# Causal attention's row maxima in chunks of four heads, spread over both sequences' steps, with a reordered first stage

## The reference

```
h = layernorm(layernorm(x)); h = causal depthwise conv of width 3 (h); q, k, v = split(h @ attn_w)   # 16 heads of 8 dims
q, k = rotary(q), rotary(k)
scores = einsum('bhqd,bhkd->bhqk', q, k) / sqrt(8)
scores = where(causal, scores, -1e30)
p = softmax(scores)
x = x + einsum('bhqk,bkhd->bqhd', p, v) @ proj_w
x = x + moe(layernorm(x))          # 4 experts, the best one for each row
```

## Time and profile before

| | |
|---|---|
| runs, us | 349.03, 351.30, 351.62 (median 351.3) |
| span of the profiled execution, first to last instruction | 346.5 us |
| time of that execution outside the span | not shown by the page; the three runs are 2.5, 4.8 and 5.1 us above the span |
| TensorE busy | 321.4 us, 93% |
| VectorE busy | 240.7 us, 69% |
| ScalarE busy | 215.8 us, 62% |
| GpSimd busy | 121.6 us, 35% |
| shares of the chain that ended last | TensorE 58%, VectorE 25%, ScalarE 10%, issue 4% |

### The profile page before, as it was taken

The page is one execution under the profiler, slowest core; times in us unless marked ns, Lnnn a source line. Parts: engine busy times, 40 slices in busy tenths (PEclk is TensorE's granted clock), DMA queues, the critical chain, the costliest instruction groups (busy, mean ns, idle before and its releaser), DMA issues.

```text
span 346.5 us, 6818 instructions
## 1 busy us (share of the span) xinstructions
PE 321.4 (93%) x2406; PEld 228.1 (66%) x2406; DVE 240.7 (69%) x607; ACT 215.8 (62%) x633; POOL 121.6 (35%) x151
## 2 busy tenths in 40 slices
PE   7888999998999998988999999998999999999885
PEld 2336887664566544435654898995688687877774
DVE  4987766594899977852651464368788877887575
ACT  1478886165237364565668744855766676686994
POOL 3525563101630033330522161410586535535300
PEclk9999999999999999999999999999999999999999
DMA  7690000057777300009002002300100000000002
GB/s 207 204 264 2 2 0 2 6 161 218 214 240 195 81 2 0 2 9 340 25 8 78 0 17 70 84 2 1 55 15 18 0 2 0 3 1 0 2 0 63
DMA packets 21591, 22.46 MB, mean 65 GB/s; under 512 B 3606, under 2 KB 18358, under 8 KB 21558
## 3 DMA queue, kind: packets, MB, share of 16 engines
q1 hardware_dynamic: 19750, 19.93, 19.8%
q0 software_dynamic: 512, 1.05, 1.0%
q10 hardware_dynamic: 1296, 1.05, 0.9%
HBM read 14.22 MB, written 7.60 MB: 63 GB/s over the span
## 4 chain that ended last, share of the span: by engine, by line
PE 58%; DVE 25%; ACT 10%; issue 4%; DMA 1%; POOL 1%; ACTq 0%; DVEq 0%; POOLq 0%
PE PS L1312 49%; DVE mB L835 9%; PE PS L1366 6%; ACT big L1122 3%; ACT big L1288 3%; DVE big L669 2%; DMA X<-in_x 1%; DVE XN L625 1%; DVE big L642 1%; DVE mraw L634 1%; ACT big L1096 1%; DVE U L625 1%; DVE stats L614 1%; DVE mraw L658 1%; ACT big L1240 1%
## 5 line engine op out<-in xcount | busy, mean ns | idle before, releaser
L1312 PE MATMUL PS<-big 128*128 128x128 f32 (+10 forms) x592 | 94.7, 308 | 6.7 <-DVE big L642 1.7
L1312 PEld LDWEIGHTS PS<-big 128*128 128x128 f32 (+3 forms) x592 | 58.0, 150 | 38.3 <-issue 11.3
L511 POOL TENSOR_TENSOR big<-big,urec 128x1024 f32<-128x1024 f32 x24 | 45.6, 1898 | 62.8 <-DVE urec L676 45.6
L1122 ACT ACTIVATE big<-big 128x154 f32<-128x154 f32 x192 | 60.4, 319 | 6.7 <-DVE big L669 5.0
L1240 ACT ACTIVATE big<-PS 128x1024 f32<-128x1024 f32 (+3 forms) x64 | 42.2, 704 | 25.5 <-PE PS L1312 25.1
L835 DVE TENSOR_REDUCE mB<-PS 128x2 f32<-128x256 f32 (+5 forms) x90 | 50.1, 624 | 7.2 <-PE PS L1312 7.2
L1096 ACT ACTIVATE big<-PS 128x1280 f32<-128x1280 f32 (+2 forms) x30 | 32.6, 1091 | 32.5 <-PE PS L1366 30.0
L1312 PE MATMUL PS<-cstb 128*128 128x128 bf16 x192 | 37.8, 220 | 0.0
L1312 PE MATMUL PS<-kkC,XT 128*128 128x462 f32 (+1 forms) x96 | 36.0, 510 | 1.7 <-DVE big L669 1.7
L499 POOL TENSOR_TENSOR rstd<-ve,minus_half 128x4 f32<-128x4 f32 (+2 forms) x13 | 13.2, 1016 | 69.0 <-DVE ve L620 69.0
L1122 ACT ACTIVATION_READ_ACCUMULATOR big<-big 128x1 f32 x192 | 36.3, 189 | 0.0
(11 more groups left out here) (192 smaller groups left out, 489.4 us busy)
## 6 DMA issues: line engine op xcount, KB each, us to landing
scr_qk<-big SPq DMA_DIRECT2D x12, 384.0 KB, 3.5
big<-scr_qk SPq DMA_DIRECT2D x16, 288.0 KB
big<-in_wv SPq DMA_DIRECT2D x1, 2048.0 KB, 8.1
scr_x<-zrow SPq DMA_DIRECT2D x2, 448.0 KB, 6.5
scr_y<-big SPq DMA_DIRECT2D x2, 448.0 KB, 3.6
X<-in_x ACTq DMA_DIRECT2D x2, 256.0 KB, 3.8
big<-in_A_WoT ACTq DMA_DIRECT2D x1, 512.0 KB, 4.7
cw<-in_C_Wk SPq DMA_DIRECT2D x1, 512.0 KB, 5.3
```

Of the source, the lines that this page charges most:

```text
L511: pool.tensor_tensor(pn[:, 0:GH * P].rearrange("p (h k) -> p h k", h=GH), Pt[u % 3][:, :, 0:KM], r.to_broadcast([P, GH, KM]), ALU.mult).th ...
L1122: i = act.activation(Pt[u % 3][:, h, :], Pt[u % 3][:, h, :], ACT.Exp, accum_out=usum[:, u % 3, h:h + 1])
L1312: return pe.matmul(o, lhsT, rhs, start=start, stop=stop)
```

## The change

The maxima are made final by chunks c = 0..7 of four heads (8 m each) instead of by sequence. Only the first 20 m (`M0`) come before the steps; the other 44 are spread over steps 0 to 21 as a ring of 66 entries, three to a step: an m with one or two tiles of columns is one entry for both heads, a wider one is two entries. The ring has two banks (5 and 6). The reductions negate. GpSimd splits each chunk into three bf16 parts, one bf16 matmul turns the three together, ScalarE copies them, and SyncE stores them. The folds of `PREC` go with m = 2..19, one each. The five `hold_clock` matmuls between the sequences are gone. Sequence 0 is now transposed and normalised four heads at a time too, in steps 5, 9, 13, 17, and `turn_outputs` and `normalise_first` are gone. ScalarE issues the two loads of expert weights. In stage A the reciprocal of unit u-1 comes between the maximum and the clamp of unit u, transposes come before values, values are three units behind, VectorE makes the second half of the queries, constants are spread over units 0 to 4, nine of the `hold_clock` matmuls are gone, `turn("b")` comes before folds 3 to 5, folds 6 to 8 come after the first `queries_keys`, which no longer waits for the last `add_tile`.

```diff
@@ block.vector, units_A @@
+                        if u >= 1:
+                            row_sums(u - 1)
                         own.wait()
                         own(dve.tensor_scalar(umax[:, u % 2, :], mraw[:, u % 2, :], LEAST, None, ALU.max))
...
-                    if u >= 1:
-                        v = u - 1
-                        dve.wait_ge(unit_exp["A"], v + 1)
-                        dve.reciprocal(urec[:, v % 3, :], usum[:, v % 3, :]).then_inc(unit_rec["A"], 1)
-                    if u >= 4:
-                        add_tile("A", u - 4)
+                    else:
+                        row_sums(u - 1)
+                    if u >= 3:
+                        add_tile("A", u - 3)
...
@@ block.tensor, units_A @@
+                    if 2 <= u <= NT + 1:
+                        turn_weights("A", u - 2)
                     if u == 2:
                         pe.wait_ge(q4_ready, B)
                         hold_clock(OUT_BANK["A"], 8)
-                    elif u == 3:
-                        hold_clock(OUT_BANK["A"], 5)
-                    if u >= 4:
-                        weigh_values("A", u - 4, vwAm, vwAr)
-                    if 2 <= u <= NT + 1:
-                        turn_weights("A", u - 2)
+                    if u >= 3:
+                        weigh_values("A", u - 3, vwAm, vwAr)
...
             def second_gap():
+                turn("b", XN, (0,))
                 fold_C(F_UNIT[0], F_UNIT[1])
-                turn("b", XN, (0,))
...
-                else:
-                    pe.wait_ge(tile_added["A"], NT)
...
+        M0 = 20
+        M_STEPS = 22
+        S_CHUNK = (None, 0, 3, 7, 11, 15, 20, 23)
+        S_SPLIT = {2: 2, 6: 3, 10: 4, 14: 5}
+        RING = []
+        for m in range(M0, 64):
+            RING += [(m, (0, 1))] if m % QT < QT // 2 else [(m, (0,)), (m, (1,))]
+        def ring_bank(k):
+            return 5 + k % 2
...
+            def split_maxima(c):
+                pool.tensor_copy(mp[:, c % 2, 0], m).then_inc(m_part, 1)
+                pool.tensor_tensor(mr[:], m, mp[:, c % 2, 0], ALU.subtract).then_inc(part_step, 1)
+                pool.tensor_copy(mp[:, c % 2, 1], mr[:]).then_inc(m_part, 1)
+                pool.tensor_tensor(mp[:, c % 2, 2], mr[:], mp[:, c % 2, 1], ALU.subtract).then_inc(m_part, 1)
...
+            def ring_scores(k):
+                if k < 2:
+                    pe.wait_ge(s_max, M0)
+                else:
+                    pe.wait_ge(s1_max, k - 1)
...
             late = F_LATE
-            for m in range(32):
+            for m in range(M0):
                 scores_for_maximum(m)
-                if m >= 3 and m % 2 == 1 and late < F_BETWEEN:
+                if m >= 2 and late < len(PREC):
                     fold_C(late, late + 1)
                     late += 1
-            hold_clock(7, 5)
-            turn_maxima(0)
+                if late == F_MAX:
+                    turn_maxima(0)
...
-                    if s < S_MAX:
-                        scores_for_maximum(M_MERGE + 2 * s + pair)
-                if s >= 1 and s != 16:
+                    if s < M_STEPS:
+                        ring_scores(3 * s + pair)
+                if s >= 1:
                     outputs(s - 1)
...
+                if s < M_STEPS:
+                    ring_scores(3 * s + 2)
+                if s in S_CHUNK:
+                    turn_maxima(S_CHUNK.index(s))
+                if s >= 5 and s % QT == 1 and s != 21:
+                    turn_group(*divmod((s - 5) // QT, 4))
```

More of the change, by code:

```diff
@@ L251, in program @@
         F_VALUES = 42
-        F_BETWEEN = 46
+        F_MAX = 45
         def prec_jobs():
@@ L381, in program, with first_bank, ring_done @@
         PREA = [(kind, b, k) for b in range(B) for kind, k in (("vw", 0), ("vw", 1), ("vr", 0))]
[L383 to L388, removed]
+        def first_bank(m):
+            return (0, 2, 5)[(m - M0) % 3]
+        RING = []
+        for m in range(M0, 64):
+            RING += [(m, (0, 1))] if m % QT < QT // 2 else [(m, (0,)), (m, (1,))]
+        assert len(RING) == 3 * M_STEPS
+        def ring_bank(k):
+            return 5 + k % 2
+        def ring_done(c):
+            return sum(m < M_CHUNK * (c + 1) for m, _ in RING)
         def y_bank(n):
@@ L1370, in units_A @@
             def units_A(between):
-                for u in range(NT + 4):
+                for u in range(NT + 3):
                     if u < NT:
@@ L1546, in _, with turn_maxima, scores_of @@
             pe.wait_ge(consts_ready, 2)
-            def turn_maxima(b):
-                pe.wait_ge(*((s1_max, 2 * (64 - M_MERGE)) if b else (s_max, 32)))
-                if b:
-                    pe.wait_ge(m_part[0], 1)
-                pe.transpose(PS[0:HB * QT, 6, 0:P], mB[:, b].rearrange("p h t -> p (h t)"), ident).then_inc(m_turned, 1)
-            def scores_for_maximum(m):
+            def turn_maxima(c):
+                pe.wait_ge(m_part, 3 * (c + 1))
+                if c == 0:
+                    pe.wait_ge(preC_act, sum(j[2] for j in PREC[:F_MAX - 1]))
+                elif c == 1:
+                    pe.wait_ge(preC_act, N_PREC)
+                elif c == 2:
+                    pe.wait_ge(rwc_ready, 2)
+                elif c <= 5:
+                    pe.wait_ge(y_norm, c - 2)
+                elif c == 6:
+                    pe.wait_ge(attn_added, 1)
+                elif c == 7:
+                    pe.wait_ge(routed, 1)
+                mm(PS[0:3 * HG * QT, LN_BANK, M_AT:M_AT + P], mp[:, c % 2].rearrange("p a n -> p (a n)"), identb).then_inc(m_turned, 1)
+            def scores_of(b, h, qt, o):
+                w = (qt + 1) * P
+                mm(o, qs[b][0:SPLIT, h, qt * P:w], ks[b][0:SPLIT, h, 0:w], stop=False)
+                return mm(o[:, w - P:w], identb, mask_qk, start=False)
+            def scores_for_maximum(m):
+                hp, qt = divmod(m, QT)
+                if m % M_CHUNK == 0:
+                    pe.wait_ge(stack_ready[0][m // M_CHUNK], 32)
+                if m >= 3:
+                    pe.wait_ge(s_max, m - 2)
+                for j in range(2):
+                    i = scores_of(0, 2 * hp + j, qt, PS[:, first_bank(m) + j, 0:(qt + 1) * P])
+                i.then_inc(s_mm, 1)
+            def ring_scores(k):
+                m, heads = RING[k]
                 b, n = divmod(m, 32)
```

407 lines of the change are left out of this document (210 added, 197 removed).

## The result

The changed kernel took 344.51, 344.60, 345.59 and 347.59 us, median 345.1, beside 349.03, 349.48, 351.30 and 351.62 us (median 350.4) of the kernel before: ratio 0.9875, 95% interval [0.983, 0.9921], 1.25% faster. The forecast was 349.4 us, 0.6% faster, with "within 1%" likelier than "faster"; the interval reaches from 0.8 to 1.7%. The time lies in the forecast's range (344.5 to 353.5), but near its lower end.

What follows compares the result with a forecast made beforehand. TensorE's work was taken as nearly the bound everywhere. The terms -1.9 - 8.2 + 6.8 + 1.35 = -1.95 brought the span from 346.5 to 344.6 us; with 4.8 added, the median was 349.4, range 344.5 to 353.5.

Steps and rivals of the forecast that it cites:

- Stage A, -1.9: From the start to the second turn: 1.9 us gained, ends nothing and 3.2.
- The loop: Stage A: exponentials, reciprocal, clamp and subtractions form a cycle of 4.5 us a unit, longer than TensorE's 4.26.
- Ahead of the steps, -8.2: First maximum's matmul to first step: 20.6 us instead of 28.8, 8.2 gained, ends 9.8 and 6.2.
- Steps, +6.8: Steps 0 to 23: 62.8 us instead of 56.0, 6.8 lost, with 0.65 a period for all waits.
- the three terms: Steps 16 to 19, added to a period: masks 0.9 us, the normalised turn 0.5, the projection 1.0.
- Tail, +1.35: Behind step 24's first exponential: places known later and the bias matmul moved in, 1.35 us lost, ends 0 and 2.2.
- the 0.9: Tail: TensorE meets the 1.65 us later places of sequence 0's rows late by about 0.9 us.
- The waits vanish: Rival, steps: TensorE's lead absorbs the ring's waits (3.6 us) and half of step 20's block (0.9): 344.9 us; chance 0.26.
- the block of step 20: VectorE's addition and statistics, 2.8 us in one piece in step 20, of which TensorE sees 1.9 us as a wait.
- Two banks are too few: Rival, steps: ring entries wait behind VectorE's copy and normalisation, 1.25 us more a period: 356.3 us; chance 0.12.
- stage A gives nothing: Rival, stage A: a unit really takes 4.7 us through signals between engines, the 1.9 gained goes: 351.3 us; chance 0.12.
- The clock falls: Rival, stage A: without fillers the clock halves for one unit, 4.26 us doubles: 353.7 us; chance 0.03.

Runs made afterwards that it cites:

- The repeat: The changed kernel run again without any edit: median 347.8 us, ratio 0.9890 to the kernel before.
- the maxima alone: The changed kernel with the first stage as before, so only the maxima by chunks are new: 350.2 us, ratio 0.9945 to the kernel before.
- the reciprocal back: The changed kernel with stage A's reciprocal back behind the subtractions: 355.3 us, ratio 1.0102 to the kernel before.
- the folds back: The changed kernel with the second turns' folds where they were before the change: 346.8 us, ratio 0.9849 to the kernel before.
- stage A's fillers back: The changed kernel with the nine filler matmuls of the first stage put back: 348.3 us, ratio 0.9931 to the kernel before.
- the seventh: The changed kernel with eight unread matmuls where TensorE waits 1.67 us in step 21: 345.2 us, ratio 0.9864 to the kernel before.
- the kernels with fillers: The changed kernel with fillers in step 21, 345.2 us; the changed kernel with 24 maxima ahead of the steps and fillers in step 29, 344.4 us.

## Why the prediction was right and wrong

**Stage A, -1.9, measured -2.5 (-2.9 from the first maximum).** The loop was right: 4.46 us a unit. Wrong were two sizes. I let unit 7 end 0.3 us later than before, which my own terms did not give (1.2 lost, 1.4 given back); from unit 0's first maximum to unit 7's it took 31.19 us after and 31.47 before, 0.3 earlier, because the constants that left unit 0 gave back 1.1 (4.40 for 5.53) and the six units behind it cost 0.85 instead of 1.2. And the wait for the normalised rows, 1.2 in the sum, was 0.63. The stretch from queries to second turn (16.2 us) was as forecast. Wrong, too, was to book the reciprocal's new place as a cost alone: with it back in its old place the first m comes 5.8 us later. The sum did not depend on it.

**Ahead of the steps, -8.2, measured -8.35.** Right as a sum, 20.42 us for 20.6, with parts that cancel: TensorE is busy for 19.63 instead of 19.0, and waits for 0.8 instead of 1.6, since fold 45 does not wait.

**Steps, +6.8, measured +6.9.** Right as a sum, with errors that cancel. TensorE's idle time in a period was 0.28, not 0.65, so two banks were enough, but its work was larger: 9.5 to 9.6 us a period, and 39.5 instead of 38.8 us for steps 0 to 15. Steps 16 to 19 took 11.25 instead of 11.9 (9.7 and the three terms add up to 12.1), with no idle time at all. Steps 20 to 23 took 12.16 for 12.1; the wait in step 21 was 1.67 for 1.9. The forecast holds for an execution at full clock: with a dip the steps take 64.3 us, +8.4.

**Tail, +1.35, measured +0.6 in the first trace, about +1.05 in the others.** The places came 0.7 us later, not 1.65, and TensorE did not meet this (no idle time at 187.27): the 0.9 was wrong. The bias matmul took 0.42, for 0.5. The repeat's trace has a wait of 0.42 us ahead of the outputs in step 29, which the first has not.

**From the span to the time.** This step was furthest off: I added 4.8 us to the span, because the median of before lay so far above its profiled span. Runs lie 1.7 to 2.3 us above their own spans. The profiled execution of before, at full clock, was shorter (346.5) than all its later runs on chip 11 (347.0 to 352.9). The profiled run of the changed kernel beat the forecast by 4.8 us: 2.9 of them lie here, 1.9 in the span. As a difference the forecast was -1.95 us of span; measured are -3.8 in the first traces, and -5.3 and -3.9 us between the medians. So the time fell into the range by its width, and the gain was about twice the forecast.

**The rivals.** "The waits vanish" named nearly the measured time (344.9), by luck: it takes all of its 4.5 us from the steps, and the steps gave none. Waits in the ring were shorter (0.28 for 0.65 a period), but TensorE's work was longer by about as much, and the block of step 20 was not hidden at all. "Two banks are too few" is refuted by 0.28 us a period, "stage A gives nothing" by every trace with the whole new stage (first m 2.6 us earlier or more). "The clock falls" had 0.03 and the wrong place: I argued from one trace in which TensorE was idle for 2.2 of 9.7 us at full clock that longer gaps do no harm. They do, in most executions: six traces have the wait of 1.67 us in step 21 unfilled (the first, its repeat, the maxima alone, the reciprocal back, the folds back, stage A's fillers back), and all but the first show a clock of 0.50 there or right behind it; the seventh, with the wait filled, stays at 1.00. The first is also the only one that is not known to be from chip 11. The Trainium skill (TensorE: Matmul & The Clock Gate, Part 1) says that the array falls to half rate after idling and, of the slow stretch at a kernel's start, that it differs from run to run of one kernel. These runs agree with the first, with 1.5 us lost a dip in steps 20 to 23, and show that a stretch in the middle of a kernel differs from run to run as well.

Open: the kernel before has spans of 347.0 to 350.1 us at full clock on chip 11, two to three times the spread of the kernels with fillers (343.0 to 344.1 and 341.7 to 343.2). Part of what varies lies behind the slots' transposes: that stretch, which no run changes, took from 154.8 to 157.7 us in the fourteen traces. The long ones have waits for VectorE (0.62 and 0.91 us with the reciprocal back) that the changed kernel's repeat has not. Why they come is not known.

## What to carry to other kernels

A wait of TensorE can cost twice: here 1.67 us by itself and, in most executions, 1.5 us more by the stretch at half clock behind it. Look at the mean granted clock of every run, not at one profile. Where a wait cannot be removed, unread matmuls can hold the clock, as long as they take no longer than the wait: five of them in stage A, where nothing waited for so long, cost 1.1 us. Measure the kernel before against itself: here it differed by 0.4%. When instructions change places for two engines at once, walk the whole loop over all engines: the move that seems to cost may be the one that feeds the next.

## What the runs showed that I had not expected

Eight matmuls of 0.22 us in a wait of 1.67 us brought all six runs to full clock, where none of the repeat's six had been. The clock's fall is not decided by the gap alone: the same 1.67 us passed at 1.00 in one trace and came with a fall in five. And two queues further on, a delay of VectorE's statistics by some 5.5 us came out as 3.57 us on TensorE, by way of 3.23 us of normalisation on GpSimd.
